# Fewer filler matmuls in the steps of a recurrence on TensorE

## The chip, the cores and the metric

The kernel runs on one core of a Trainium2 chip. The time is the device time of one execution in microseconds; lower is better. In the rows, PE is TensorE's matmuls, PEld its weight loads, DVE VectorE, ACT ScalarE, POOL GpSimd, SP SyncE.

## What is computed

The reference is two layers. Each is x + s·silu(g), on x of 16 sequences, 256 positions and 128 features, after a layer norm. In layer 0, s comes from a recurrence over the 256 positions, and g from a mixture of 8 experts (top 2, with a capacity). In layer 1, s is attention with 16 heads and g a mixture of 160 experts. The part around the change is the scan of layer 0:

```python
def step(carry, inp):
    h_ssm, h_rnn = carry
    bxt, dxt, gxt, iht = inp
    h_ssm = jax.nn.silu(h_ssm @ A.T + bxt)
    hh = h_rnn @ W_hh.T + b_hh
    i_r, i_z, i_n = jnp.split(iht, 3, axis=-1)
    h_r, h_z, h_n = jnp.split(hh, 3, axis=-1)
    r = jax.nn.sigmoid(i_r + h_r)
    z = jax.nn.sigmoid(i_z + h_z)
    n = jnp.tanh(i_n + r * h_n)
    h_rnn = (1.0 - z) * n + z * h_rnn
```

Every step needs the state of the step before, so the 256 steps are a chain.

## The kernel before, in words

States are kept transposed, 128 features by 16 sequences, in `hist_g` (the GRU state) and `hist_s` (the SSM state), one slice for each step.

**One step** (`step(t)`, written once for each engine). PE waits for the state (`rnn_ready`), then issues four f32 matmuls of 16 columns: L748 (reset gate), L750 (candidate), L751 (update gate) and L753 (SSM). An f32 matmul of this kind shows in the trace as two passes. ACT answers L748 with a tanh (`th_r`, L521), L753 with a tanh (`th_zv`, L523), and later makes the candidate (`cand`, L526). DVE does the rest in small operations: `mixn` L1216, `pren` L1218, `sumn` L1220, `omz` L1222, `zg` L1223, `hist_s` L1225, `newn` L1229, and last the new state, `hist_g` L1231, for which PE's next L748 waits. While they work, PE adds the inputs of the next step into the accumulators through matmuls with an identity: `input_r` (L739) once `th_r` has been read, and `input_zv` (L742) once `th_zv` and `hist_s` are done. PE runs its instructions in the order written.

**Fillers.** `keep_warm(n)` (L735) issues n bf16 matmuls of 512 columns on a tile of zeros; nothing reads their result. Sixteen stand ahead of the first step. In a plain step there are four behind L753 and two behind `input_r`.

**Three stretches.** The 256 steps run as 40 plain steps, then 160 steps with expert work, then 56 plain steps. In the middle stretch, a unit of four steps also runs one tile of 256 rows through an expert of layer 0; there are 40 units (8 experts, 5 tiles each). Two callbacks put that work into PE's order: `early` behind L753 and `late` behind `input_r`. By step of the unit they are:

- first step: `up(0)`, then `up(1)`
- second: `up(2)`, then `down(0)`
- third: `up(3)`, then `down(1)`
- fourth: `down(2)` with `turn_rows` (the transposes of the next tile, L774), then `down(3)`

`up` (L784) is one f32 matmul of 256 columns, `down` (L793) two of 128 columns. ACT makes a GELU (L540) from every `up`, between its tanhs, and waits for earlier `down`s before it overwrites their input. DVE moves the finished tile out (L1241) behind the fourth step, ahead of the next step's `mixn`. These steps have one filler each, behind `early`.

Beside the recurrence POOL scatters rows into DRAM in the first stretch and gathers them back in the third. Behind it come the outputs of the scan (L839 to L844, f32 matmuls of 128 columns) and layer 1.

Of the kernel before, what the change touches and what calls it, by code (L numbers as in the profile page):

```python
# [54 lines left out]
def build(nc, x, gin_w, half_w, misc_w, cols, rows, b2, w1, b1, w2,  # L55
          attn_w, attn_cols, attn_rows, router, router_row, w_gate, w_down, shared_gate, shared_down,
          jcols, sel_w, iotas, out):
    with ExitStack() as ctx:
# [638 lines left out]
        def _(pe):  # L697
# [34 lines left out]
            def keep_warm(n):  # L732

                for _ in range(n):
                    nc.tensor.matmul(ps_y[:, 1, :], warm_b[:, 0:P], warm_b[:, 0:512], start=True, stop=True)  # L735

            def input_r(t):

                nc.tensor.matmul(ps_r[:, 0:16], ident, gin[:, 0, :, t], start=True, stop=False, skip_group_check=True)  # L739

            def input_zv(t):
                nc.tensor.matmul(ps_zv[:, 0:32], ident, gin[:, 1:3, :, t], start=True, stop=False,  # L742
                                 skip_group_check=True)

            def step(t, early=None, late=None):

                pe.wait_ge(rnn_ready, t + 1)
                nc.tensor.matmul(ps_r[:, 0:16], whr, hist_g[:, :, t], start=False, stop=True,  # L748
                                 skip_group_check=True).then_inc(r_done, 1)
                nc.tensor.matmul(ps_n[:, 0:16], whn, hist_g[:, :, t], start=True, stop=True).then_inc(n_done, 1)  # L750
                nc.tensor.matmul(ps_zv[:, 0:16], whz, hist_g[:, :, t], start=False, stop=False, skip_group_check=True)  # L751
                pe.wait_ge(ssm_ready, t + 1)
                nc.tensor.matmul(ps_zv[:, 16:32], aT, hist_s[:, :, t], start=False, stop=True,  # L753
                                 skip_group_check=True).then_inc(zv_done, 1)
                if early:
                    early()
                keep_warm(4 if early is None else 1)

                pe.wait_ge(thr_ready, t + 1)
                input_r((t + 1) % T)  # L760
                if late:
                    late()
                else:
                    keep_warm(2)
                pe.wait_ge(thzv_ready, t + 1)
                pe.wait_ge(ssm_ready, t + 2)
                input_zv((t + 1) % T)
# [30 lines left out]
            def unit(g, ep, wbuf):  # L798
                def last_early():
                    down(g, ep, wbuf, 2)  # L800
                    turn_rows(g + 1)

                t = STEPS_BEFORE + g * 4
                step(t, lambda: up(g, ep, wbuf, 0), lambda: up(g, ep, wbuf, 1))
                step(t + 1, lambda: up(g, ep, wbuf, 2), lambda: down(g, ep, wbuf, 0))
                step(t + 2, lambda: up(g, ep, wbuf, 3), lambda: down(g, ep, wbuf, 1))
                step(t + 3, last_early, lambda: down(g, ep, wbuf, 3))
# [775 lines left out]
```

## Time and profile before

| | |
|---|---|
| Time, median of 3 runs | 2050.67 us (2048.13 to 2051.21) |
| The profiled execution | 2045.78 us, of which the span of the instructions is 2044.0 us |
| PE busy | 1820.5 us, 89% of the span, 14389 matmul passes |
| DVE, ACT, POOL busy | 1273.6, 887.8, 625.9 us |
| Mean granted TensorE clock | 0.936 of full |
| Chain that ended last | PE 68%, DMA 12%, DVE 10%, issue 6%, ACT 3% |

The granted clock of TensorE is shown as a share of its full 2.4 GHz; it has two levels in this trace, 1.00 (2.4 GHz) and 0.50 (1.2 GHz), and what lies between them is a stretch that had both. Ends of matmuls are modelled, so the distance between the starts of two matmuls says more than the length shown for one. Records of a few matmuls are missing.

### The profile page before, as it was taken

The page shows a single profiled execution, that of the slowest core. Times are in us where ns is not written, and L with a number is a line of the kernel's source. Part 1 is how long each engine was busy: PE and PEld are TensorE (multiplying, and loading weights), DVE is VectorE, ACT ScalarE, POOL GpSimd, SP SyncE. Part 2 cuts the span into 40 slices and gives each one's busy share as a digit, 9 for nine tenths or more (in the row PEclk, how much of TensorE's full clock was granted, in tenths as well). Part 3 has the DMA queues.
Part 4 walks back from the last instruction along what each step waited for, and adds up shares of the span by engine and source line. Part 5 has one row for each costly group of instructions (what it writes and reads, how often), then busy time and mean ns, then how long its engine had stood idle before and what let it go on. Part 6 is the DMA issues. An engine that isn't in the chain of part 4 may idle for free.

```text
span 2044.0 us, 49776 instructions
## 1 busy us (share of the span) xinstructions
PE 1820.5 (89%) x14389; PEld 1625.6 (80%) x14390; DVE 1273.6 (62%) x4624; ACT 887.8 (43%) x2899; POOL 625.9 (31%) x661
## 2 busy tenths in 40 slices
PE   4789999999999999377999999799999988888896
PEld 2467999999997778256999999688887877787785
DVE  4344445445444442888888888555554777677675
ACT  2212344444442221233666666444445555555453
POOL 0065000000005600005677776000000555555551
PEclk9889999999999995587999999899999899999996
DMA  9611011111101100301111111355555111111111
GB/s 375 251 41 44 18 36 36 38 38 36 36 26 41 44 0 0 131 32 39 47 50 50 52 51 47 144 172 174 167 171 160 44 40 39 39 40 40 39 40 52
DMA packets 153497, 149.29 MB, mean 73 GB/s; under 512 B 16931, under 2 KB 134374, under 8 KB 153062
## 3 DMA queue, kind: packets, MB, share of 16 engines
q1 hardware_dynamic: 130820, 100.98, 14.9%
q0 software_dynamic: 21760, 46.18, 7.7%
q10 hardware_dynamic: 866, 1.51, 0.2%
q8 instruction: 24, 0.39, 0.1%
q14 instruction: 27, 0.22, 0.0%
HBM read 70.95 MB, written 77.66 MB: 73 GB/s over the span
## 4 chain that ended last, share of the span: by engine, by line
PE 68%; DMA 12%; DVE 10%; issue 6%; ACT 3%; POOL 1%; DVEq 1%; ACTq 0%; POOLq 0%; SPq 0%
DMA rows_g<-ys_dram,slot 11%; PE ps_y L735 8%; PE ps_t L940 5%; PE ps_y L793 4%; PE ps_up L1050 4%; PE ps_up L784 4%; PE ps_t L1063 4%; PE ps_up L916 3%; PE ps_y L929 3%; PE ps_t L751 3%; PE ps_t L753 3%; PE ps_rec L750 3%; PE ps_rec L748 3%; PE ps_rec L1020 2%; PE ps_rec L884 2%
## 5 line engine op out<-in xcount | busy, mean ns | idle before, releaser
L479 POOL DMA_INDIRECT rows_g<-ys_dram,slot x256 | 242.6, 948 | 487.7 <-DMA ys_dram<-slots_y 306.4
L623 ACT ACTIVATE probs<-ps_up,negmax 128x256 f32<-128x256 f32 x512 | 240.7, 484 | 326.3 <-DVE negmax L1457 326.3
L469 POOL DMA_INDIRECT xs_dram<-xn_tok,slot x256 | 249.8, 976 | 314.0 <-DVE slot L1359 216.7
L940 PE MATMUL ps_t<-v_sb,probsT 128*128 128x64 f32 x2048 | 260.7, 271 | 2.0 <-DVE ctx_sb L1440 1.4
L940 PEld LDWEIGHTS ps_t<-v_sb,probsT 128*128 128x128 f32 x2048 | 252.1, 194 | 4.4 <-issue 4.3
L735 PE MATMUL ps_y<-zeros 128*128 128x512 bf16 x752 | 219.3, 381 | 0.0
L1216 DVE SCALAR_TENSOR_TENSOR mixn<-ps_rec,cols_sb,th_r 128x16 f32<-128x16 f32 x256 | 59.9, 234 | 244.0 <-PE ps_rec L750 142.1
L1457 DVE TENSOR_REDUCE negmax<-ps_up 128x2 f32<-128x512 f32 x256 | 164.8, 686 | 32.3 <-PE ps_up L916 31.8
L916 PE MATMUL ps_up<-kT,qT 64*128 64x256 f32 x1536 | 129.1, 301 | 61.4 <-DVE kT L1413 60.9
L916 PEld LDWEIGHTS ps_up<-kT,qT 64*128 64x128 f32 x1536 | 103.0, 191 | 82.2 <-issue 61.5
L929 PE MATMUL ps_y<-misc,probs 128*128 128x128 f32 x1024 | 163.6, 283 | 0.6 <-ACT probs L623 0.5
L521 ACT ACTIVATE th_r<-ps_rec 128x16 f32<-128x16 f32 x256 | 46.3, 181 | 219.1 <-PE ps_rec L748 219.1
L739 PEld LDWEIGHTS ps_rec<-gin,misc 128*128 128x128 f32 x514 | 97.7, 190 | 46.3 <-DVE slot_to L1204 13.7
L1400 DVE SCALAR_TENSOR_TENSOR xn_tok<-rows_g,w,xn_tok 128x128 f32 (+1 forms) x224 | 78.7, 351 | 86.2 <-DMA rows_g<-ys_dram,slot 66.8
L929 PEld LDWEIGHTS ps_y<-misc,probs 128*128 128x128 f32 x1024 | 114.6, 143 | 18.9 <-ACT probs L623 1.6
L884 PE MATMUL ps_rec<-xr,w_high 128*128 128x256 f32 x520 | 111.5, 308 | 12.6 <-DVE xr L1406 12.6
L793 PE MATMUL ps_y<-w_sb,h_sb 128*128 128x128 f32 x640 | 110.5, 295 | 0.0
L623 ACT ACTIVATION_READ_ACCUMULATOR probs<-ps_up,negmax 128x1 f32 x512 | 109.8, 214 | 0.0
L784 PE MATMUL ps_up<-slots_xT,w_sb 128*128 128x256 f32 x320 | 108.5, 421 | 0.0
L1431 DVE COPY probsT<-ps_y 128x512 f32<-128x512 f32 x128 | 88.1, 688 | 27.1 <-PE ps_y L929 27.0
L540 ACT ACTIVATE h_sb<-ps_up,b_sb 128x256 f32<-128x256 f32 x160 | 75.8, 474 | 65.8 <-PE ps_y L793 65.7
L431 POOL DMA_DIRECT2D w_sb<-w x8 | 4.6, 569 | 318.1 <-PE ps_y L793 318.1
(241 smaller groups left out, 4457.6 us busy)
## 6 DMA issues: line engine op xcount, KB each, us to landing
xs_dram<-zeros SPq DMA_DIRECT2D x52, 512.0 KB, 5.9
slots_x<-xs_dram SPq DMA_DIRECT2D x88, 256.0 KB, 3.0
ys_dram<-slots_y SPq DMA_DIRECT2D x84, 256.0 KB, 2.5
slots_x<-xs_dram SPq DMA_DIRECT2D x41, 128.0 KB, 2.2
ys_dram<-slots_y SPq DMA_DIRECT2D x40, 128.0 KB, 1.8
gate<-w_gate SPq DMA_DIRECT2D x1, 5120.0 KB, 20.5
down<-w_down SPq DMA_DIRECT2D x1, 5120.0 KB, 15.2
w_sb<-w POOLq DMA_DIRECT2D x16, 256.0 KB, 4.8
```

Source lines behind the costliest of these rows:

```text
L469: nc.gpsimd.indirect_dma_start(xs_dram, bass.IndirectOffsetOnAxis(ap=slot[:, n, k:k + 1], axis=0), xn_tok[:, n, :], None).then_inc(scatter ...
L479: nc.gpsimd.indirect_dma_start(rows_g[:, i % 16, :], None, ys_dram, bass.IndirectOffsetOnAxis(ap=slot[:, i // TOPK1, i % TOPK1:i % TOPK1 + ...
L623: nc.scalar.activation(probs[:, a, i, :], ps_s[a][:, T * i:T * i + T], ACT.Exp, bias=negmax[:, a, i:i + 1], accum_out=sums[:, j % 4, i, a: ...
L735: nc.tensor.matmul(ps_y[:, 1, :], warm_b[:, 0:P], warm_b[:, 0:512], start=True, stop=True)
L739: nc.tensor.matmul(ps_r[:, 0:16], ident, gin[:, 0, :, t], start=True, stop=False, skip_group_check=True)
L784: nc.tensor.matmul(ps_up[j % 2][:, 0:256], w1_sb[:, wbuf, P * j:P * j + P], slots0_xT[:, :], start=True, stop=True).then_inc(up_ready, 1)
L793: last = nc.tensor.matmul(ps_y[:, 0, P * s:P * s + P], h_sb[:, j % 2, P * s:P * s + P], w2_sb[:, wbuf, j, :], start=(j == 0 and s == 0), s ...
L884: last = nc.tensor.matmul(dst, left[a_], right[b_], start=(k == 0), stop=(k == 2))
L916: last = nc.tensor.matmul(ps_s[a][:, T * i:T * i + T], qT[rows_a, j % 2, a_, P * i:P * i + P], kT[rows_a, j % 2, b_, :], start=(k == 0), s ...
L929: last = nc.tensor.transpose(ps_y[:, a, T * kc + P * i:T * kc + P * i + P], probs[:, a, i, P * kc:P * kc + P], ident)
L940: last = nc.tensor.matmul(ps_ctx[:, P * i + HD * a:P * i + HD * a + HD], probsT[:, a, kc, P * i:P * i + P], v_sb[:, j % 2, kc, HD * a:HD * ...
L1457: V.tensor_reduce(negmax[:, a, :], ps_s[a][:, :].rearrange("p (i t) -> p i t", i=2), AX_X, ALU.max, negate=True).then_inc(max_ready, 1)
```

## The change

The two calls of `keep_warm` in `step` on TensorE are changed. In plain steps there are four fillers behind L753 as before, and one behind `input_r` where there were two. In steps with an `early` callback, the one filler is gone. The sixteen ahead of the first step stay, and no other engine's code changes.

```diff
@@ -754,14 +754,15 @@
                                  skip_group_check=True).then_inc(zv_done, 1)
                 if early:
                     early()
-                keep_warm(4 if early is None else 1)
+                else:
+                    keep_warm(4)
 
                 pe.wait_ge(thr_ready, t + 1)
                 input_r((t + 1) % T)
                 if late:
                     late()
                 else:
-                    keep_warm(2)
+                    keep_warm(1)
                 pe.wait_ge(thzv_ready, t + 1)
                 pe.wait_ge(ssm_ready, t + 2)
                 input_zv((t + 1) % T)
```

## Rows read from the trace of the kernel before

**Rows 1.** The page: granted clock in 40 equal slices, 51.1 us each, tenths

```profile
PEclk9889999999999995587999999899999899999996
```

**Rows 2.** Windows: stretch in us, then busy (x) of PE, PEld, DVE, ACT, POOL, PEclk, DMA

```profile
136.00:160.00 24.00, 24.00 (x177) 18.85 (x176) 11.69 (x78) 5.95 (x30) 18.21 (x20) 1.00 0.15 52
400.00:500.00 100.00, 99.69 (x780) 93.55 (x778) 49.61 (x329) 43.60 (x169) 2.56 (x4) 1.00 0.13 36
```

**Rows 3.** The page's groups by line: the fillers

```profile
L735 PE MATMUL ps_y<-zeros 128*128 128x512 bf16 x752 | 219.3, 381 | 0.0
```

**Rows 4.** Timeline of one plain step: start us, length us, engine, line

```profile
141.24 0.38 PE L748 MATMUL ps_rec<-hist_g,halfw 128*128 x2
...
141.65 0.18 ACT L521 ACTIVATE th_r<-ps_rec 128x16 f32<-128x16 f32 x1 [1.36 <-PE ps_rec L748]
...
142.13 1.02 PE L735 MATMUL ps_y<-zeros 128*128 128x512 bf16 x4
...
143.13 0.59 PE L735 MATMUL ps_y<-zeros 128*128 128x512 bf16 x2
143.18 0.19 DVE L1231 SCALAR_TENSOR_TENSOR hist_g<-zg,newn 128x16 f32 x1
...
143.56 0.31 PE L742 MATMUL ps_t<-gin,misc 128*128 x2
...
143.70 0.37 PE L748 MATMUL ps_rec<-hist_g,halfw 128*128 x2
```

**Rows 5.** Timeline of one unit, from its fourth step to the next fourth step

```profile
403.48 0.38 PE L748 MATMUL ps_rec<-hist_g,halfw 128*128 x2
...
406.14 0.38 PE L748 MATMUL ps_rec<-hist_g,halfw 128*128 x2
...
406.41 0.42 DVE L1241 TENSOR_TENSOR slots_y<-ps_y,b_sb 128x256 f32<-128x256 f32 x1 [0.64 <-PE ps_y L793]
...
407.09 0.23 DVE L1216 SCALAR_TENSOR_TENSOR mixn<-ps_rec,cols_sb,th_r 128x16 f32<-128x16 f32 x1 [0.25 <-issue]
...
408.28 0.19 DVE L1231 SCALAR_TENSOR_TENSOR hist_g<-zg,newn 128x16 f32 x1
...
408.60 0.37 PE L748 MATMUL ps_rec<-hist_g,halfw 128*128 x2
...
411.02 0.38 PE L748 MATMUL ps_rec<-hist_g,halfw 128*128 x2
...
411.24 0.47 ACT L540 ACTIVATE h_sb<-ps_up,b_sb 128x256 f32<-128x256 f32 x1 [0.68 <-PE ps_y L793]
...
411.61 0.17 ACT L521 ACTIVATE th_r<-ps_rec 128x16 f32<-128x16 f32 x1
...
413.46 0.37 PE L748 MATMUL ps_rec<-hist_g,halfw 128*128 x2
```

**Rows 6.** Windows (columns of rows 2): around falls of the clock, and one at full level

```profile
768.00:782.00 14.00, 14.00 (x49) 11.31 (x50) 2.11 (x6) 2.20 (x6) 0.00 (x0) 0.50 0.00 0
904.00:906.00 2.00, 1.58 (x8) 0.75 (x8) 1.96 (x10) 0.00 (x0) 0.00 (x0) 1.00 0.01 4
906.00:908.00 2.00, 1.16 (x7) 0.57 (x6) 2.00 (x11) 0.00 (x0) 0.00 (x0) 0.85 0.03 8
908.00:910.00 2.00, 1.59 (x7) 0.54 (x7) 2.00 (x10) 0.00 (x0) 0.00 (x0) 0.50 0.00 0
1720.00:1734.00 14.00, 11.13 (x104) 10.49 (x104) 10.65 (x28) 7.14 (x25) 8.24 (x9) 1.00 0.15 38
```

**Rows 7.** Timeline: the same instructions at the low and at the full level

```profile
112.76 0.15 PEld L735 LDWEIGHTS ps_y<-zeros 128*128 128x128 bf16 x1 [0.28 <-issue]
113.19 0.15 PEld L735 LDWEIGHTS ps_y<-zeros 128*128 128x128 bf16 x1 [0.28 <-issue]
...
1768.23 1.00 PE L940 MATMUL ps_t<-v_sb,probsT 128*128 128x64 f32 x8
...
1778.33 1.80 PE L940 MATMUL ps_t<-v_sb,probsT 128*128 128x64 f32 x8
```

## The prediction

> **What bounds the kernel now.** I read the page's clock line first. The granted clock stands at its upper level through nearly all of the recurrence, which runs from about 116 us to 755 us, and falls to about half behind it [rows 1]. Then the windows: in a stretch of plain steps PE is busy 24.00 of 24.00 us, and in the steps with expert work 99.69 of 100.00 us, both at a granted clock of 1.00, the 2.4 GHz level; DVE and ACT are busy at most half of the time [rows 2]. So in both kinds of step PE's own order of work sets the pace, and the fillers are a part of that order. They are 752 matmuls [rows 3]: 16 ahead of the first step, 6 in each of the 96 plain steps (576), 1 in each of the 160 steps with expert work.
>
> Last I read one step of each kind for what would bound it without PE. A plain step takes 143.70 - 141.24 = 2.46 us from L748 to the next L748. The chain through the other engines: the tanh L521 starts 0.41 us behind L748, and the write of the new state, L1231, starts 1.94 us behind it (143.18 - 141.24) [rows 4]. The shortest way from the start of that write to the next L748 that I find is 408.60 - 408.28 = 0.32 us [rows 5]. The loop of dependencies is therefore 1.94 + 0.32 = 2.26 us, 0.20 us shorter than the step.
>
> **The change, part by part.**
>
> One filler takes (143.56 - 143.13) / 2 = 0.215 us of PE's time at the upper level [rows 4]. 256 go: 96 from the plain steps and 160 from the steps with expert work.
>
> *Plain steps at the upper level.* PE's share falls to 2.46 - 0.215 = 2.245 us, the loop of dependencies of 2.26 us takes over, and a step gains 0.20 us. `input_zv` is asked for 0.2 us earlier, still behind the end of `hist_s`, so no wait comes new in its place. 96 steps would give 19.2 us.
>
> *Steps with expert work at the upper level.* A unit takes 413.46 - 403.48 = 9.98 us [rows 5]; its steps are 2.66, 2.46, 2.42 and 2.44 us, beginning with the fourth. Less 0.215 each, PE needs 2.45, 2.25, 2.21 and 2.23. Against that stand the loops. The fourth step stays with PE, 2.45. In the first, DVE's eviction L1241 and what follows it hold `mixn` until 407.09, and the state is written 2.14 us behind L748, so the step stays 2.14 + 0.32 = 2.46: nothing is gained. The second has a loop of 2.26. In the third a GELU (411.24) stands ahead of `th_r`, which starts 0.59 us behind L748 in place of 0.41 [rows 4, 5]; the slack won in the second step (2.26 against 2.21) pulls the GELU forward by 0.05, so 0.13 of the delay stays and the step takes 2.39. Sum 9.56, a gain of 0.42 a unit, 16.8 us over 40 units. The bounds are 0 (each step held by such a delay) and 4 x 0.215 = 0.86 a unit, 34 us.
>
> *The clock.* This is where I expect the change to decide itself, since the fillers do no work but this. First, what the level is worth. The fillers ahead of the first step start 0.43 us apart at 0.50, against 0.215 at 1.00; eight narrow f32 passes (64 columns) take 1.80 us at 0.50 and 1.00 us at 1.00 [rows 4, 7]. Taking off the tail of the last (one takes about 0.42 and 0.27), that is 0.20 against 0.10 us apart. So wide and narrow work both take twice as long. A unit after the change is 9.98 - 0.86 = 9.12 us of PE work, 18.24 at the lower level (1.2 GHz); a plain step is 2.245, or 4.49. The loops through ACT and DVE keep their 2.3 us or so and are hidden, so PE alone would set the pace.
>
> Then, whether it falls. Every step has four recurrent matmuls and the two input matmuls, of 16 or 32 columns, which fill about 1.17 us of PE's time (142.13 - 141.24 = 0.89 for the four, 143.70 - 143.56 = 0.14 for each of the two others) and move hardly anything through the array. What is left of a unit, 9.98 - 4 x (1.17 + 0.215) = 4.44 us, is its eight expert blocks and a transpose, about half a microsecond each, and the filler is the only other wide work in a step. Without it, nothing wide is left but the blocks. The rows show that a PE without gaps is no safety: at 768 to 782 us it is busy 14.00 of 14.00 us with 128-column f32 matmuls and stays at 0.50. At 904 to 908 us PE works with short gaps (busy 1.58 and 1.16 of 2.00 us) at the full level, and the level is lost within the second of these windows (0.85, then 0.50). On the other side, at 1720 to 1734 us PE is idle 2.87 of 14 us between dense blocks and keeps 1.00 [rows 6]. Steps with expert work after the change lie between these: no gaps, but the smallest share of wide work of any long stretch that now stands at 1.00, and 40 units in which one fall is enough. I take the fall. I place it four units in (bounds: the first unit, or halfway, the 20th).
>
> Then, whether it rises again. The rise at 116 us came out of 16 fillers back to back. A slow unit has no such run, and a slow plain step has five fillers in 4.49 us where narrow passes take the rest; the work at 768 us, denser than either, didn't bring it back. I take it as lost until the end of the recurrence. Behind it nothing changes: the outputs of the scan stand at 0.50 already.
>
> The Trainium skill speaks against this. "TensorE: Matmul & The Clock Gate", in the table of "Why this matters for your kernels", has the clock fall in idle gaps between bursts and asks for none that are long. PE has no gap here, so by that rule the clock holds, the sum is the first rival's, about 2015 us; the stretch at 768 us doesn't agree with reading it that way.
>
> *The sum.* 40 plain steps x -0.20 = -8.0. Four units x -0.42 = -1.7. 36 units x (18.24 - 9.98) = +297.4. 56 plain steps x (4.49 - 2.46) = +113.7. Together +401 us. The profiled execution's own time is 2045.8 us, so 2447; the median of the runs shown is 4.9 us above that execution, so **2452 us**. A fall in the first unit gives some 25 us more, one after 20 units 137 us less.
>
> **The rivals.**
>
> *The clock holds (faster).* Then the gains are all there is: 19.2 + 16.8 = 36 us, and the time is 2051 - 36 = 2015 us, 1997 to 2031 with the bounds. For it: the present steps with expert work stay at 1.00 for 400 us with one filler of 0.215 us in 2.5, and the steps also become shorter, so that the wide blocks lie closer. It decides on whether the level is ever lost among the 160 steps; if not once, this side wins.
>
> *The clock falls, but comes back in the last 56 plain steps.* For it: five fillers a step are more wide work than the expert steps have. Then -8.0 - 1.7 + 297.4 - 11.2 = +276 us, 2327 us.
>
> *It goes up and down.* If a slow unit can bring it back, say half of the units are slow: 20 x 8.26 = +165, less 8.0, 8.4 and 11.2 = +138 us, 2189 us. Against it: a slow unit spreads the same wide work over twice the time.
>
> *The fillers cost nothing.* A step would stay as it is, 2051 us, if some wait filled the place of each. Only the first step of a unit shows such a wait.
>
> **How the numbers follow.** Fall without return 0.61; return in the last stretch 0.11; up and down 0.08; clock holds 0.18; no change 0.02. The likeliest gives 2452 us, its own range 2310 to 2490 (a fall after 20 units; a fall at once, with up to 15 us of waits at the slow level). The range has to reach down over the return (2327) and the up and down (2189), so 2150 to 2490; left out are the clock that holds and no change, 0.20. Faster by over 0.2% (about what a measurement of this kernel can tell from no change) is the holding clock, 0.18; within 0.2% 0.02; slower 0.80.
>
> **What would show it.** 496 fillers in the trace. The first plain steps 2.26 us from L748 to L748 at 1.00; if 2.46, the loop of dependencies was misread. PEclk 0.50 from somewhere in the first units to the end of the recurrence, the units 18.2 us long and the last plain steps 4.49 us, PE without gaps; the recurrence ends near 1156 us in place of 755. If the clock line stands at 1.00 there, the forecast is wrong by its main term, and units of 9.56 us test the rest.

## The result, and the profile after

| | before | after |
|---|---|---|
| Median time | 2049.4 us (4 runs, 2042.5 to 2051.2) | 2433.4 us (4 runs, 2431.0 to 2436.8) |
| Ratio, 95% interval | | 1.188 (1.185 to 1.191) |
| Span of the profiled execution | 2044.0 us | 2429.2 us |
| Mean granted TensorE clock | 0.936 | 0.754 |

The changed kernel is slower by 19%. The forecast was 2452 us. The page of the changed kernel, its busy line of PE, the clock in 40 slices (60.7 us each here) and three of its groups:

```profile
PE 2202.3 (91%) x14094; PEld 1988.7 (82%) x14134; DVE 1270.3 (52%) x4624; ACT 870.8 (36%) x2899; POOL 626.4 (26%) x661
...
PEclk9797555555555555555556999999999999999997
...
L735 PE MATMUL ps_y<-zeros 128*128 128x512 bf16 x457 | 185.6, 517 | 7.0 <-issue 6.4
L794 PE MATMUL ps_y<-w_sb,h_sb 128*128 128x128 f32 x640 | 191.7, 455 | 0.0
L785 PE MATMUL ps_up<-slots_xT,w_sb 128*128 128x256 f32 x320 | 190.5, 699 | 0.0
```

PE has fewer instructions than before and is busy for 382 us more. The mean length of a filler goes from 381 ns [rows 3] to 517 ns. The x457 is short of 496 by records that are missing; the weight loads of the same line number 496. The clock line says where the time is: from the fifth slice through the twenty-first it stands at half. The recurrence ends inside the nineteenth slice (at 1143 us), and up to there the clock stood at full before [rows 1].

The same in windows, busy (x) of PE, PEld, DVE, ACT, POOL, then PEclk and DMA:

```profile
136.00:160.00 24.00, 23.72 (x175) 19.32 (x178) 12.65 (x84) 6.33 (x32) 18.21 (x20) 1.00 0.15 52
206.00:215.00 9.00, 8.82 (x58) 7.85 (x57) 4.29 (x30) 3.79 (x15) 0.00 (x0) 0.89 0.06 17
215.00:220.00 5.00, 5.00 (x24) 5.00 (x25) 1.11 (x8) 1.33 (x5) 0.00 (x0) 0.50 0.00 0
400.00:500.00 100.00, 100.00 (x426) 96.04 (x427) 28.27 (x189) 23.62 (x98) 1.28 (x2) 0.50 0.07 18
960.00:1100.00 140.00, 136.49 (x536) 107.22 (x553) 37.27 (x263) 15.81 (x98) 24.32 (x26) 0.50 0.05 13
```

The fourth row answers to the steps with expert work in [rows 2]: 100 us hold 426 matmul passes of PE, which is busy all the time, where they held 780. The level is lost within the second row, in the first unit: the unit's first L748 starts at 207.59, and the mean of 0.89 over 206 to 215 us puts the fall at about 213 us. It stays lost to the end of the recurrence.

The writes of the state mark the stretches (timeline of DVE, the 40th, 200th and last step):

```profile
206.81 0.19 DVE L1232 SCALAR_TENSOR_TENSOR hist_g<-zg,newn 128x16 f32 x1
...
900.98 0.19 DVE L1232 SCALAR_TENSOR_TENSOR hist_g<-zg,newn 128x16 f32 x1
...
1143.27 0.19 DVE L1232 SCALAR_TENSOR_TENSOR hist_g<-zg,newn 128x16 f32 x1
```

The same writes in the trace before, the 40th and the 200th (the last is at 754.56):

```profile
214.58 0.19 DVE L1231 SCALAR_TENSOR_TENSOR hist_g<-zg,newn 128x16 f32 x1
...
616.51 0.19 DVE L1231 SCALAR_TENSOR_TENSOR hist_g<-zg,newn 128x16 f32 x1
```

The first one is at 118.60 there and at 116.75 here. So the first stretch takes 90.1 us in place of 96.0, the 160 steps with expert work 694.2 in place of 401.9, and the last 56 steps 242.3 in place of 138.0: -5.9 + 292.3 + 104.3 = +391 us. The span grew by 385; the other -5 us lie outside the recurrence, where the code is the same.

One slow unit and one slow plain step (timeline, only PE's rows that mark them):

```profile
500.64 0.59 PE L748 MATMUL ps_rec<-hist_g,halfw 128*128 x2
...
502.35 1.20 PE L785 MATMUL ps_up<-slots_xT,w_sb 128*128 128x256 f32 x2
...
503.34 0.45 PE L739 MATMUL ps_rec<-gin,misc 128*128 x2
...
504.91 0.59 PE L748 MATMUL ps_rec<-hist_g,halfw 128*128 x2
...
518.14 0.59 PE L748 MATMUL ps_rec<-hist_g,halfw 128*128 x2
...
1049.87 0.59 PE L748 MATMUL ps_rec<-hist_g,halfw 128*128 x2
...
1054.19 0.59 PE L748 MATMUL ps_rec<-hist_g,halfw 128*128 x2
```

A unit takes 518.14 - 500.64 = 17.50 us against 9.98, a plain step 4.32 against 2.46. The four recurrent matmuls take 502.35 - 500.64 = 1.71 us against 0.89, the block of `up` 503.34 - 502.35 = 0.99.

### The profile page after: what moved, and what is told of

Its sections match the earlier page's. It is cut to its first block, busy times and chain, and to the rows that moved or that the text cites. A ratio compares the mean times of both kernels' runs of the same rounds, so it can differ in the third digit from the quotient of the medians.

```text
span 2429.2 us, 49225 instructions
## 1 busy us (share of the span) xinstructions
PE 2202.3 (91%) x14094; PEld 1988.7 (82%) x14134; DVE 1270.3 (52%) x4624; ACT 870.8 (36%) x2899; POOL 626.4 (26%) x661
## 4 chain that ended last, share of the span: by engine, by line
PE 73%; DMA 10%; DVE 8%; issue 5%; ACT 2%; POOL 0%; DVEq 0%; ACTq 0%; POOLq 0%; SPq 0%
DMA rows_g<-ys_dram,slot 9%; PE ps_y L794 7%; PE ps_up L785 7%; PE ps_y L735 7%; PE ps_t L753 4%; PE ps_t L751 4%; PE ps_rec L750 4%; PE ps_t L941 4%; PE ps_rec L748 4%; PE ps_up L1051 3%; PE ps_t L1064 3%; PE ps_up L917 3%; PE ps_t L742 3%; PE ps_y L930 2%; PE ps_rec L739 2%
## 5 line engine op out<-in xcount | busy, mean ns | idle before, releaser
L739 PEld LDWEIGHTS ps_rec<-gin,misc 128*128 128x128 f32 x514 | 155.7, 313 | 61.2 <-issue 15.5
L735 PE MATMUL ps_y<-zeros 128*128 128x512 bf16 x457 | 185.6, 517 | 7.0 <-issue 6.4
L794 PE MATMUL ps_y<-w_sb,h_sb 128*128 128x128 f32 x640 | 191.7, 455 | 0.0
L785 PE MATMUL ps_up<-slots_xT,w_sb 128*128 128x256 f32 x320 | 190.5, 699 | 0.0
L794 PEld LDWEIGHTS ps_y<-w_sb,h_sb 128*128 128x128 f32 x640 | 155.3, 332 | 0.0
L742 PEld LDWEIGHTS ps_t<-gin,misc 128*128 128x128 f32 x514 | 142.7, 306 | 13.2
L523 ACT ACTIVATE th_zv<-ps_t 128x32 f32<-128x32 f32 x256 | 50.4, 197 | 254.8 <-PE ps_t L753 254.8
L748 PE MATMUL ps_rec<-hist_g,halfw 128*128 x512 | 141.1, 355 | 0.5
L753 PE MATMUL ps_t<-hist_s,halfw 128*128 x512 | 141.4, 356 | 0.0
```

Source lines behind the costliest of these rows:

```text
L785: nc.tensor.matmul(ps_up[j % 2][:, 0:256], w1_sb[:, wbuf, P * j:P * j + P], slots0_xT[:, :], start=True, stop=True).then_inc(up_ready, 1)
L794: last = nc.tensor.matmul(ps_y[:, 0, P * s:P * s + P], h_sb[:, j % 2, P * s:P * s + P], w2_sb[:, wbuf, j, :], start=(j == 0 and s == 0), s ...
```

## The experiments

The theory was the one of the prediction: the lost fillers of the steps with expert work lose the clock level, and the level alone makes the time. The rivals: the plain steps lose it; something else slows the tail; only the number of fillers counts; any work that keeps PE busy does as well as a filler.

**Each part of the change alone.** First the plain steps alone (`plain5_expert1`), by putting the one filler back:

```diff
                 if early:
                     early()
-                else:
-                    keep_warm(4)
+                keep_warm(4 if early is None else 1)
```

> Only the plain steps change: five fillers there, one in each step with expert work as before. If the loss comes from the fillers taken out of the steps with expert work, the granted clock stays at 1.00 through the recurrence and only the gain of the plain steps is left: in the profile of the changed kernel three plain steps of four take 2.25 us and the fourth about 2.45, mean 2.30 against 2.46, so 96 x 0.16 = 15 us less than before, about 2034 us. If five fillers in a plain step were already too few for the clock, it would fall in the first 40 steps or the last 56, and the time would be above 2100 us.

Measured: 2032.3 us (median of 5), before 2042.6 us on the same chip, ratio 0.994 (0.991 to 0.997). The clock holds through the recurrence, which is 621.2 us long from the first write of the state to the last, against 636.0. That is the 15 us that were expected; the medians differ by 10.

Then the steps with expert work alone (`plain6_expert0`), the changed kernel with `keep_warm(2)` behind `input_r`:

> Only the steps with expert work change: none there, six fillers in a plain step as before. Theory: the clock falls within the first units, and the 160 steps take about 694 us in place of 402, +292. What the last 56 steps do is open: if six fillers a step bring the level back soon, they take about 140 us and the time is about 2345 us; if not, they take 56 x 4.7 = 265 us and it is about 2465 us. If the loss needed both parts of the change, the time stays near 2035 to 2050 us.

Measured: 2307 us, one execution. That is 38 us under the 2345 expected for a quick return of the level, and 32 of them are in the 160 steps, which took 661.9 us and not 694. Windows of the two, plain5_expert1 first:

```profile
400.00:500.00 100.00, 99.67 (x778) 93.42 (x778) 49.58 (x327) 43.66 (x169) 2.56 (x4) 1.00 0.13 37
640.00:720.00 80.00, 79.96 (x593) 64.78 (x593) 41.70 (x280) 20.77 (x105) 44.28 (x47) 1.00 0.15 39
```

```profile
220.00:250.00 30.00, 29.91 (x235) 28.75 (x234) 16.17 (x105) 13.73 (x54) 0.00 (x0) 1.00 0.09 26
250.00:260.00 10.00, 9.99 (x74) 9.58 (x73) 5.14 (x33) 4.22 (x17) 0.00 (x0) 0.90 0.09 26
300.00:800.00 500.00, 500.00 (x2116) 479.30 (x2115) 142.58 (x944) 116.94 (x486) 6.41 (x10) 0.50 0.07 20
880.00:900.00 20.00, 20.00 (x91) 14.89 (x90) 5.25 (x37) 2.46 (x15) 12.96 (x14) 0.59 0.16 42
900.00:1020.00 120.00, 120.00 (x878) 94.19 (x877) 58.34 (x389) 28.79 (x146) 47.49 (x51) 1.00 0.11 28
```

The loss belongs to the steps with expert work; five fillers in a plain step hold the level and gain 10 us by themselves. Without a filler in the expert steps the level went at about 258 us here, after more than four units, and with six fillers in a plain step it came back at about 896 us, some 20 us into the last stretch. So the two parts do meet in one place: the sixth filler is what brings the level back in the tail, as far as one execution shows it. With five it didn't return by itself in the 242 us of the changed kernel's tail, nor in the tails of the four kernels below that reach it at the low level (fill_0111, fill_1010, half_width, narrow_filler; 242 to 243 us each).

The four units at full level also let the first half of the sum be read. These are the L748 of the second of them, from its first step to the first step of the next unit:

```profile
223.62 0.39 PE L748 MATMUL ps_rec<-hist_g,halfw 128*128 x2
...
226.05 0.37 PE L748 MATMUL ps_rec<-hist_g,halfw 128*128 x2
...
228.32 0.37 PE L748 MATMUL ps_rec<-hist_g,halfw 128*128 x2
...
230.68 0.37 PE L748 MATMUL ps_rec<-hist_g,halfw 128*128 x2
...
233.18 0.39 PE L748 MATMUL ps_rec<-hist_g,halfw 128*128 x2
```

Steps of 2.43, 2.27, 2.36 and 2.50 us, 9.56 together. The other three units took 9.66 (the first), 9.54 and 9.54 us.

**The level alone, in the tail** (`burst_before_tail`): the changed kernel, with one line ahead of the last loop of plain steps.

```diff
+            keep_warm(16)
             with pe.Fori((STEPS_BEFORE + STEPS_MOE) // 4, T // 4) as u:
                 for j in range(4):
                     step(u * 4 + j)
```

> The changed kernel with 16 fillers back to back ahead of the last 56 plain steps (about 7 us at the low level). If the level is the whole cause of the slow tail, the burst brings it back to 1.00 and five fillers a step hold it, as they do in the first 40 steps: the tail takes 56 x 2.30 = 129 us in place of 242, and the time is 2433 - 113 + 7 = about 2327 us. If five fillers do not hold it there, or something else slows the tail, the time is 2433 to 2440 us.

Measured: 2323 us, one execution. Windows and PE's timeline at the burst:

```profile
895.00:902.00 7.00, 7.00 (x33) 6.78 (x33) 1.74 (x14) 1.40 (x6) 0.00 (x0) 0.50 0.00 0
902.00:906.00 4.00, 4.00 (x13) 1.45 (x11) 0.42 (x1) 0.00 (x0) 0.68 (x1) 0.58 0.11 33
906.00:1030.00 124.00, 123.78 (x913) 100.06 (x911) 63.66 (x424) 31.72 (x160) 59.78 (x64) 1.00 0.13 34
```

```profile
901.82 5.37 PE L735 MATMUL ps_y<-zeros 128*128 128x512 bf16 x16
```

The tail with the burst takes 136.0 us, as expected (129 + 7), in place of 242.3. 5.4 us of fillers buy back 110 us. The same five fillers a step that could not lift the level hold it once it is there.

**Busy, but narrow** (`narrow_filler`): in each step with expert work, behind `early`,

```diff
+            def keep_busy():
+
+                for _ in range(2):
+                    nc.tensor.matmul(ps_y[:, 1, 0:16], warm_b[:, 0:P], warm_b[:, 0:16], start=True, stop=True)
...
                     early()
+                    keep_busy()
                 else:
                     keep_warm(4)
```

> The changed kernel, with two bf16 matmuls of 16 columns in place of the one filler of 512 columns in each step with expert work: about the same time on PE's queue (0.2 us, by its weight loads), next to no columns. If the clock follows how wide the work is, it falls in the first units as without fillers, and the time is 2433 us or somewhat more (two weight loads of bf16 at the low level in each of 160 steps, up to 0.2 us each, 2433 to 2470 us). If it follows whether PE is kept busy, it holds, and the time is about 2035 us.

Measured: 2466 us, one execution; the level went at about 225 us.

```profile
208.00:222.00 14.00, 13.94 (x114) 12.81 (x113) 6.67 (x45) 5.94 (x23) 0.00 (x0) 1.00 0.07 21
222.00:226.00 4.00, 4.00 (x31) 3.49 (x30) 2.21 (x16) 1.88 (x8) 0.00 (x0) 0.85 0.10 30
300.00:900.00 600.00, 600.00 (x2670) 556.68 (x2670) 161.86 (x1073) 133.53 (x553) 6.42 (x10) 0.50 0.06 19
```

PE was busy 13.94 of 14 us just before the fall. The pair turned out shorter at the full level than the filler that it stands for (about 0.1 us), so it is no equal in time; but PE's work had no gap to speak of, 0.06 us in 14. With the wide filler in the same place the level held in all 28 executions of the kernel before and of plain5_expert1 that were timed. At the low level it costs (18.45 - 17.49) / 4 = 0.24 us a step, which is why this is the slowest kernel of all.

**Number or place.** Two kernels with three fillers in a unit of four steps. They differ in which step goes without. `step` takes the number as an argument:

```diff
-            def step(t, early=None, late=None):
+            def step(t, early=None, late=None, fill=0):
...
                     early()
+                    keep_warm(fill)
                 else:
                     keep_warm(4)
```

In `fill_1110` the first three steps of the unit are called with `fill=1`, in `fill_0111` the last three. The fourth step is the one with the transposes and `down(2)` in `early`.

> Five fillers in a plain step; in a unit of four steps with expert work one filler in the first three and none in the fourth, which has a transpose and two blocks besides. If what counts is the weakest stretch of a unit and not the number of fillers, the clock holds at 1.00 through the recurrence, the fourth step gives up its 0.215 us on PE, and a unit takes 9.77 us: 40 x 0.21 = 9 us less than the run with one filler in each step (2032), about 2024 us, ratio to before 0.99. If any filler less loses the level, the time is 2200 to 2430 us.

Measured: 2024.5 us (median of 6, 2019.2 to 2027.6), before 2042.4 us on the same chip, ratio 0.992 (0.989 to 0.994).

> The same number of fillers, 120 in the steps with expert work, but the first step of each unit is the one without. This step follows the two narrow stretches at the turn of the unit and gains nothing in time by it. If the place decides, the clock falls at some point of the 160 steps, most likely in the first half, and does not return: 2250 to 2440 us. If only the number of fillers counts, it does what the run without the fourth step's filler does.

Measured: 2371 us, one execution. Windows, fill_1110 first:

```profile
400.00:500.00 100.00, 99.53 (x779) 93.29 (x778) 51.11 (x332) 44.14 (x171) 2.56 (x4) 1.00 0.13 38
```

```profile
300.00:340.00 40.00, 39.52 (x308) 37.11 (x307) 19.80 (x131) 17.57 (x68) 1.28 (x2) 1.00 0.14 38
340.00:344.00 4.00, 4.00 (x19) 3.54 (x18) 1.12 (x8) 1.51 (x5) 0.00 (x0) 0.51 0.03 9
400.00:800.00 400.00, 400.00 (x1643) 369.65 (x1643) 106.36 (x704) 87.01 (x362) 3.84 (x6) 0.50 0.06 18
```

With the same 120 fillers, one placing holds for all 40 units and the other loses the level at 340 us, in the 14th unit. The number alone does not decide, as far as these runs go: fill_1110 held in all six of its executions, but fill_0111 ran once, and the next kernel shows that one program can do both. If both placings lost the level equally often, a loss in the one run of fill_0111 and none in the six of fill_1110 would come up in at most 6 of 100 such trials. So the place very likely counts, and a repeat of fill_0111 would have to settle it.

**Two fillers in four steps** (`fill_1010`, `fill=1` in the first and third step):

> Five fillers in a plain step; in a unit one filler in the first and in the third step. If the clock holds, a unit takes 9.55 us by the steps measured at the full level without any filler in the run with six fillers in a plain step (9.54), and the time is about 2032 - 40 x 0.44 = 2015 us. If two fillers in four steps are too few, it falls somewhere in the 160 steps, later than without any (at 213 us there), and the time is between 2050 and 2430 us and differs from execution to execution.

Measured, four executions of the one program: 2007.9, 2457.6, 2458.1 and 2464.1 us. The mean granted clock was 0.940 in the first of these and 0.751 or 0.752 in the other three, so the level went in three of them and not in the fourth. In the profiled one it went in the first unit:

```profile
208.00:214.00 6.00, 5.95 (x44) 5.08 (x42) 2.86 (x21) 2.56 (x11) 0.00 (x0) 1.00 0.09 25
214.00:220.00 6.00, 5.88 (x33) 5.34 (x31) 1.89 (x13) 2.06 (x7) 0.00 (x0) 0.63 0.01 1
```

The best time of the study and its second worst come from the same instructions. "Later than without any" was not borne out: in the profiled execution the fall, at about 215 us, is as early as in the changed kernel. What differed between the executions is not shown.

**Half the width** (`half_width`): in place of `keep_warm(fill)` one matmul of 256 columns in each step with expert work.

```diff
                     early()
+                    nc.tensor.matmul(ps_y[:, 1, 0:256], warm_b[:, 0:P], warm_b[:, 0:256], start=True, stop=True)
                 else:
                     keep_warm(4)
```

> Five fillers in a plain step; each step with expert work has one filler of 256 columns in place of 512, about 0.11 us of PE. If the clock holds, a unit takes 9.99 - 4 x 0.11 = 9.55 us or somewhat more and the time is about 2015 us. If half the columns are too few, the clock falls in the 160 steps, later than without any filler, and the time is 2100 to 2430 us.

Measured: 2380 us, one execution; the level was lost within this window, by its mean of 0.61 at about 322 us, later than in the changed kernel (213), as expected:

```profile
300.00:400.00 100.00, 99.77 (x501) 92.47 (x501) 32.63 (x215) 27.51 (x111) 2.56 (x4) 0.61 0.10 29
```

## Why the prediction was right, point by point

**That the clock decides: right.** The main term was the lower level in the steps with expert work and in the tail. The parts alone and the burst show it, not only the clock line: the same plain steps of the tail take 2.25 us behind the burst (2.45 once in four) and 4.32 without it. Nothing else was changed there.

**That the level does not return: right for this kernel,** and by a narrow margin in the tail. The rival "comes back in the last 56 plain steps" was right for the neighbour with six fillers. "Up and down" was seen in no run: in every trace the level fell at most once inside the recurrence, and it rose again in two kernels only, with six fillers in the tail and behind the burst. One reading behind this point was too simple. The stretch at 768 us was called denser than either kind of step, but one in four of its matmuls uses a single row of the array, as the trace before shows; no run here tells how such a matmul counts.

```profile
761.01 0.79 PE L844 MATMUL ps_t<-rows_sb,misc 1*128 1x128 f32 x2
```

**Where it falls: off.** I took it to hold for four units; it fell in the first. A unit that holds takes 9.56 us and one that doesn't 17.50, so the early fall costs (4 - 0.7) x 7.94 = 26 us against the forecast. The neighbour with the same expert steps held for more than four units, while burst_before_tail, like the changed kernel, lost the level in its first; whether the sixth filler in the plain steps ahead has a part in that is not shown. The fall lay within the bounds given (first to 20th unit). For the far bound the sum is 16 x 8.68 = 139 us less, not 137.

**The price of a slow unit: 17.50 us, not 18.24; of a slow plain step 4.32, not 4.49.** Doubling all of PE's time was a little too much. The four recurrent matmuls go from 0.89 to 1.71 us, not 1.78, and the `up` block from about 0.52 to 0.99. The prediction's own rows had said so: its narrow passes are (1.00 - 0.27) / 7 = 0.104 us apart at the full level and (1.80 - 0.42) / 7 = 0.197 at the low one, 1.9 times and not twice, and only the fillers double. The step of the sum that was mis-sized is the price of the level, by 0.74 us a unit and 0.17 a plain step, 39 x 0.74 = 29 and 56 x 0.17 = 9.5 us in all. The earlier fall gave 26 us of the first back, so that the 160 steps came to +292 us (forecast +296) is in part luck: two errors cancel. The tail came to +104 (+114), the first 40 steps to -6 (-8). Of the 19 us between 2452 and 2433, 11 are in the recurrence and 5 outside it, and the rest is the distance of the median from the profiled execution (4.9 us then, 2.4 now).

**The plain steps at the full level: nearly.** The loop of dependencies is 2.25 us, as worked out (2.26), but only in three steps of four:

```profile
124.12 0.30 PEld L748 LDWEIGHTS ps_rec<-hist_g,halfw 128*128 128x128 f32 x2 [0.17 <-issue]
```

In the fourth, at the turn of the loop, PE itself waits for nothing that the profile shows (0.17 us here), and that step takes about 2.45. Before, it did not show: PE was busy 24.00 of 24 us [rows 2], and is now busy 23.72. That the work queued on PE hid it then is argued, not tested. The mean of the first stretch is 90.1 / 39 = 2.31 us a step, a gain of 0.15 in place of 0.20.

**The steps with expert work at the full level: right.** 9.56 us a unit was worked out and 9.54 to 9.66 measured in the four units where the level held; the steps were 2.46, 2.26, 2.39 and 2.45 by the working and 2.43, 2.27, 2.36 and 2.50 in the unit shown, so small misses of both signs cancel in the sum. Had the clock held, the first rival's 36 us would probably have been close: the one execution of fill_1010 that held, with two fillers a unit, came out at 2007.9 us, 35 below its before of 2042.4.

**The rule against it.** The Trainium skill, "TensorE: Matmul & The Clock Gate", section "Why this matters for your kernels", warns of idle gaps between bursts. Two runs don't agree with reading it as the only danger: the level fell with PE busy 13.94 of 14 us before it in narrow_filler, and 29.91 of 30 us in plain6_expert0.

**A version that beats both.** fill_1110 with five fillers in a plain step: 2024.5 us against 2042.4, 0.8% less (0.6 to 1.1). It gained some 5 us in the recurrence over plain5_expert1 (616.0 against 621.2 us), where 9 were expected, so the 2024 us of the expectation was met in part by luck. Its units take 9.88 us at the median, not 9.77. The turn of the unit's loop on PE shows here too: in its trace, in the four units that begin between 268 and 298 us, the first L748 starts 0.25 to 0.28 us behind the L742 ahead of it, where the trace before has 0.14 at the same place, so some 0.1 us of the filler's 0.215 is lost again.

## What to carry to other kernels

A filler has no reader, so nothing in the computation fails when it is taken away, and its saving can be read off the timeline to within some hundredths of a microsecond; what it holds up is seen only in the granted clock. Before one is removed, work out what the whole stretch costs at the other level, since the loss (8 us a unit here) can be twenty times the gain (0.4), and look at whether anything behind it could bring the level back. If fillers cost too much, try the step with the most wide work of its own first, as in the placing that held here, keep them elsewhere, and run the result several times.

## What the runs showed of the hardware that was not expected

- The same steps keep the level at which they start. Five fillers a step held 1.00 in the first 40 steps and in the tail behind the burst, and did not lift 0.50 in 242 us of the same tail; with six it rose about 20 us into it. A slow step spreads the same matmuls over 4.32 us in place of 2.31, so this needs no memory in the clock; whether it has one is not shown.
- One program gave 2007.9 us and 2458 to 2464 us. This kernel is not a little slower on the average but takes one of two times, so one good run of it proves nothing, and the single runs of the other kernels here show only what can happen.
- Half the clock did not quite double the f32 work, narrow or wide: the four recurrent matmuls went from 0.89 to 1.71 us and the `up` block from 0.52 to 0.99, 1.9 times each. The f32 weight loads slow down as well, in the traces from 0.19 to 0.33 us each.
